# Counting edges on TensorE with the source number split by two bits instead of one

## The reference

```
e = einsum('ehd,ehd->eh', k[src], q[dst]) / sqrt(DK)
m = segment_max(e, dst);  ex = exp(e - m[dst])
z = segment_sum(ex, dst);  attn = ex / z[dst]
a = segment_sum(attn[:, :, None] * v[src], dst)
```

## Time and profile before

| | us |
|---|---|
| median of three runs | 1808.47 |
| lowest and highest run | 1805.55, 1809.08 |
| the profiled execution's own time | 1806.97 |
| its span, first to last instruction | 1805.3 |
| around the span in that execution | 1.67 |
| the stage of the change within the span | 236.4 to 315.9 |
| DVE's first and last one-hot table | 241.67 to 312.50 |
| last product to the end of its logarithm | 314.00 to 315.63 |

### The profile page before, as it was taken

How to read it: one execution, slowest core, us unless ns; L and a number is a source line. 1 busy time by engine, 2 the same in 40 slices (tenths; PEclk the granted TensorE clock), 3 DMA queues, 4 the chain that set the end, 5 groups by cost and what they waited for, 6 DMA issues and landing times. The chain is left out here.

```text
span 1805.3 us, 31339 instructions
## 1 busy us (share of the span) xinstructions
PE 1603.1 (89%) x9860; PEld 1171.5 (65%) x9860; DVE 998.6 (55%) x1981; ACT 732.4 (41%) x1641; POOL 559.7 (31%) x638
## 2 busy tenths in 40 slices
PE   2997857899999887999999999479999999898994
PEld 2555535788888555569999999455555555745662
DVE  7533379788885784610000000469999999441233
ACT  2233346666665234442222211355555555422331
POOL 6777710111100221520000000435555553233133
PEclk7999979899999996999999999679999999998997
DMA  8538810688663304567555550565555554639985
GB/s 208 117 83 267 271 45 1 184 247 234 159 163 85 82 1 175 148 218 290 208 207 205 214 193 9 145 178 163 156 154 155 156 156 112 222 80 279 358 267 185
DMA packets 146055, 305.94 MB, mean 169 GB/s; under 512 B 42493, under 2 KB 59745, under 8 KB 141221
## 3 DMA queue, kind: packets, MB, share of 16 engines
q1 hardware_dynamic: 106590, 224.70, 39.6%
q0 software_dynamic: 39360, 79.86, 16.1%
HBM read 226.47 MB, written 77.96 MB: 169 GB/s over the span
## 5 line engine op out<-in xcount | busy, mean ns | idle before, releaser
L2197 PE MATMUL acc<-prod,ohy 128*64 128x256 f32 x1056 | 248.8, 386 | 7.7 <-DVE prod L2315 7.7
L2241 ACT ACTIVATE ohy<-oh,RECS 128x64 f32<-128x64 f32 x704 | 187.1, 336 | 151.6 <-PE acc L2197 151.5
L2197 PEld LDWEIGHTS acc<-prod,ohy 128*64 128x64 f32 x1056 | 138.4, 138 | 132.3 <-issue 70.7
L2174 POOL DMA_INDIRECT rows<-up_dram,idx x176 | 167.0, 949 | 143.8 <-DVE prod L2315 101.9
L1951 DVE TENSOR_SCALAR FT<-y_ps,b2T 128x188 f32<-128x188 f32 x32 | 13.2, 414 | 323.4 <-PE y_ps L1900 323.4
L321 POOL DMA_INDIRECT rec_dram<-recs,pos x157 | 161.9, 1031 | 60.6 <-issue 49.6
L2200 PE MATMUL acc<-prod,ohy 128*64 128x256 f32 x704 | 177.3, 395 | 0.0
L1888 PE MATMUL hid_ps<-FT,W 128*128 128x188 f32 x1024 | 167.7, 325 | 0.7 <-ACT FT L1925 0.7
L2315 DVE TENSOR_TENSOR prod<-w_ps,rows 128x768 f32<-128x768 f32 x176 | 166.3, 945 | 0.0
L1888 PEld LDWEIGHTS hid_ps<-FT,W 128*128 128x128 f32 x1024 | 165.2, 192 | 0.9 <-issue 0.9
L1900 PE MATMUL y_ps<-hid,W 128*128 128x188 f32 x1024 | 164.5, 323 | 0.0
(11 more groups left out here) (401 smaller groups left out, 2907.8 us busy)
## 6 DMA issues: line engine op xcount, KB each, us to landing
W<-in_L_ffn_w SPq DMA_DIRECT2D x16, 4096.0 KB, 16.6
raw_dram<-X SPq DMA_DIRECT2D x40, 585.9 KB
X<-raw_dram SPq DMA_DIRECT2D x40, 585.9 KB
bankW_sp<-in_L_ffn_W_sp SPq DMA_DIRECT2D x2, 4096.0 KB, 23.3
h_dram<-h3e SPq DMA_DIRECT2D x22, 256.0 KB, 4.8
h<-h_dram SPq DMA_DIRECT2D x22, 256.0 KB
QF<-q_dram SPq DMA_DIRECT2D x20, 250.0 KB, 5.8
b2B<-in_L_ffn_b_sp SPq DMA_DIRECT2D x17, 256.0 KB, 7.6
```

The source lines that it names most:

```text
L2174: pool.indirect_dma_start(out=rows[:, t, :], out_offset=None, in_=up_dram, in_offset=bass.IndirectOffsetOnAxis(ap=idx[:, par, t:t + 1], ax ...
L2197: upper = lambda m: nc.tensor.matmul(acc[0:HALFB, bank, :].rearrange("p (b c) -> p b c", c=MUL)[:, m:4:3 - m, :], ohs[:, 1 + m, :], pr[:, ...
L2241: last = nc.scalar.activation(ohy[:, t % OHY, i, :], oh[:, par, t, :], ACT.Copy, scale=RECS[:, bass.ds(BATCH * g + t, 1), 4 + i])
```

## The change

The source number is split by its two lowest bits instead of its lowest one. There are four classes of sources (`CLASSES = 4`), and each has at most 313 (`FOURTH`). The one-hot of a source has 314 columns instead of 626. The key of a receiver is its place in the block plus 64 times the class, so there are 256 keys instead of 128, and `ohD` has 1024 elements for four tiles instead of 512. PE multiplies the lower 128 keys and the upper 128 keys by the same 313 columns, into the first and the second bank of the region. ACT takes the logarithm in four activations of 313 or 312 columns, each of which writes every fourth column of the masks, and clears 313 columns in each of the two banks.

```diff
-            HALFN = NODES // 2
-            WIDEN = 626
-            PARTS = [(0, 512), (512, HALFN - 512)]
+            CLASSES = 4
+            FOURTH = -(-NODES // CLASSES)
+            WIDEN = FOURTH + FOURTH % 2
...
-                ohS, ohD = sb("ohS", [128, CRING, WIDEN], F16), sb("ohD", [128, CRING // SET, 2 * HALFB, SET], F16)
-                keys_by_tile = sb("keys_by_tile", [128, 2 * HALFB, SET], F16)
+                ohS, ohD = sb("ohS", [128, CRING, WIDEN], F16), sb("ohD", [128, CRING // SET, CLASSES * HALFB, SET], F16)
+                keys_by_tile = sb("keys_by_tile", [128, CLASSES * HALFB, SET], F16)
...
-                            nc.vector.tensor_scalar(parityI[:, mine], srcI[:, mine], 1, None, ALU.bitwise_and)
-                            step(nc.vector.tensor_scalar(srcI[:, mine], srcI[:, mine], 1, None, ALU.arith_shift_right))
+                            nc.vector.tensor_scalar(classI[:, mine], srcI[:, mine], CLASSES - 1, None, ALU.bitwise_and)
+                            step(nc.vector.tensor_scalar(srcI[:, mine], srcI[:, mine], int(math.log2(CLASSES)), None, ALU.arith_shift_right))
...
-                                                    .unsqueeze(1).to_broadcast([128, 2 * HALFB, SET]), ALU.is_equal)
+                                                    .unsqueeze(1).to_broadcast([128, CLASSES * HALFB, SET]), ALU.is_equal)
...
-                                for c0, cn in PARTS:
-                                    last = nc.tensor.matmul(ps[:, bass.ds(spots[t] + c0, cn)], ohD[:, g % AHEAD, :, t],
-                                                            ohS[:, slot, c0:c0 + cn], start=False, stop=False, skip_group_check=True)
+                                for two in range(CLASSES // 2):
+                                    last = nc.tensor.matmul(ps[:, bass.ds(spots[t] + 512 * two, FOURTH)],
+                                                            ohD[:, g % AHEAD, 2 * HALFB * two:2 * HALFB * (two + 1), t],
+                                                            ohS[:, slot, 0:FOURTH], start=False, stop=False, skip_group_check=True)
...
-                            for odd in range(2):
-                                nc.scalar.activation(masks(i)[HALFB * half:HALFB * half + rows, odd:NODES:2],
-                                                     ps[HALFB * odd:HALFB * odd + rows, first:first + HALFN], ACT.Ln,
-                                                     bias=least[HALFB * odd:HALFB * odd + rows, :], scale=4.0).then_inc(logged, 1)
+                            for c in range(CLASSES):
+                                at, own = first + 512 * (c // 2), HALFB * (c % 2)
+                                nc.scalar.activation(masks(i)[HALFB * half:HALFB * half + rows, c:NODES:CLASSES],
+                                                     ps[own:own + rows, at:at + len(range(c, NODES, CLASSES))], ACT.Ln,
+                                                     bias=least[own:own + rows, :], scale=4.0).then_inc(logged, 1)
                             if b + REGIONS < BLOCKS:
-                                act.wait_ge(logged, 2 * (b + 1))
-                                nc.scalar.activation(ps[:, first:first + HALFN], zeros[:, 0:1].to_broadcast([128, HALFN]),
+                                act.wait_ge(logged, CLASSES * (b + 1))
+                                nc.scalar.activation(ps[:, first:first + REGION].rearrange("p (a n) -> p a n", n=512)[:, :, 0:FOURTH],
+                                                     zeros[:, 0:1].unsqueeze(2).to_broadcast([128, 2, FOURTH]),
                                                      ACT.Copy).then_inc(evicted, 1)
```

More of the change, by code:

```diff
@@ L729, in count_edges @@
                 nodes16 = sb("nodes16", [128, WIDEN], F16)
-                srcI, parityI = sb("srcI", [128, ETILES], I32), sb("parityI", [128, ETILES], I32)
+                srcI, classI = sb("srcI", [128, ETILES], I32), sb("classI", [128, ETILES], I32)
                 key16 = sb("key16", [128, GROUPS, EPP], F16)
-                ohS, ohD = sb("ohS", [128, CRING, WIDEN], F16), sb("ohD", [128, CRING // SET, 2 * HALFB, SET], F16)
-                keys_by_tile = sb("keys_by_tile", [128, 2 * HALFB, SET], F16)
+                ohS, ohD = sb("ohS", [128, CRING, WIDEN], F16), sb("ohD", [128, CRING // SET, CLASSES * HALFB, SET], F16)
+                keys_by_tile = sb("keys_by_tile", [128, CLASSES * HALFB, SET], F16)
                 least = sb("least", [128, 1])
@@ L755, in _ @@
                         nc.gpsimd.memset(least[:], 2.0 ** -60)
-                        nc.gpsimd.iota(keys_by_tile[:], pattern=[[1, 2 * HALFB], [0, SET]], base=0, channel_multiplier=0,
+                        nc.gpsimd.iota(keys_by_tile[:], pattern=[[1, CLASSES * HALFB], [0, SET]], base=0, channel_multiplier=0,
                                        allow_small_or_imprecise_dtypes=True)
@@ L779, in keys @@
                             step(nc.vector.tensor_copy(srcI[:, mine], RECS[:, mine, 0]))
-                            nc.vector.tensor_scalar(parityI[:, mine], srcI[:, mine], 1, None, ALU.bitwise_and)
-                            step(nc.vector.tensor_scalar(srcI[:, mine], srcI[:, mine], 1, None, ALU.arith_shift_right))
+                            nc.vector.tensor_scalar(classI[:, mine], srcI[:, mine], CLASSES - 1, None, ALU.bitwise_and)
+                            step(nc.vector.tensor_scalar(srcI[:, mine], srcI[:, mine], int(math.log2(CLASSES)), None, ALU.arith_shift_right))
                             nc.vector.tensor_copy(RECS[:, mine, 0], srcI[:, mine])
                             step(nc.vector.scalar_tensor_tensor(out=key16[:, groups_of, :].rearrange("p g t -> p (g t)"),
-                                                                in0=parityI[:, mine], scalar=float(HALFB), in1=RECS[:, mine, 1],
+                                                                in0=classI[:, mine], scalar=float(HALFB), in1=RECS[:, mine, 1],
                                                                 op0=ALU.mult, op1=ALU.add))
```

## The result

| | us |
|---|---|
| before, median of six runs taken with the changed kernel | 1809.20 (1805.55 to 1812.89) |
| after, median of six runs | 1821.95 (1817.48 to 1826.23) |
| ratio after to before | 1.0077, 95% interval 1.0058 to 1.0097 |
| profiled execution after, its span | 1817.48, 1815.9 |
| length of the stage in the profiled executions | before 79.5, after 94.5 |

A forecast was written before the change was run, and what follows sets the result against it. DVE was taken to set the pace of the stage, PE 16% and ACT about 20% behind. DVE -2.3, PE's end +0.5 and ACT's last block +0.6 sum to -1.2 us: 1807.3 us, range 1804.2 to 1813.

The forecast's parts named there:

- no gain on DVE: Rival: at the lower slope DVE's set stays at 1.51 us; +1.1 us at most, 1809.6; chance 0.15.
- the larger gain: Rival: DVE's set takes 1.35 us, whole 1804, or POOL's stall shrinks, whole 1805; chance 0.13.
- The other form of that rival: POOL's split stalls DVE's last tables 1 us in place of 2.7; sum about -3.4 us, 1805; within the 0.13.
- PE and POOL: PE's products hidden behind DVE by 0.18 us a set; POOL's tables hidden with 2.5 us of cover; stall moves later.
- That term: End of PE's work: last one-hot to last product 2.0 us in place of 1.50; +0.5 us (0 to 1.5).
- ACT: the step that failed: Four logarithms of 0.61 us, a block 3.2 us, absorbed by four regions; only the last block counts, +0.6 us.
- The point of decision: ACT delays DVE's fortieth set, which needs the sixteenth region cleared, from 3.27 us a block, 0.62 us a logarithm.
- the rival: ACT becomes the bound: writes 16 bytes apart cost a second cycle, block 4.1 us; about +13 us, 1821; chance 0.17.
- its mild form: ACT's writes cost half a cycle more: 0.70 us a logarithm, 3.6 us a block; about +3 us, 1811.

The follow-up runs named there:

- experiment 2: Changed kernel with each of the four logarithms writing its columns without a gap (masks' columns in another order): 1804.24 us, ratio 0.9986 to before.
- experiment 3: Changed kernel with the four logarithms writing every second column of half the masks (columns in another order): 1805.04 us, ratio 0.9986 to before.
- experiment 6: Changed kernel with the sources split into four ranges, so each logarithm writes adjacent columns in the right order: 1806.87 us, ratio 0.9995 to before.
- experiment 7: Changed kernel with classes 2k and 2k+1 in two banks, two logarithms a block writing adjacent pairs: 1805.97 us, ratio 0.9989 to before.
- experiment 8: Kernel with sources split into four ranges, its four logarithms reordered 0, 2, 1, 3: 1805.38 us, ratio 0.9994 to before, stage 75.8 us.
- experiment 11: Network left out: four logarithms in a row without waits, same 64 partitions or halves in turns: 1.74 against 2.14 us without a gap.
- experiment 1: Network left out: single activations and copies at several write steps; 313-column logarithm 0.532 us at two words, 0.667 at three, 803 ns at four.
- Experiment 4: Kernel before with its two logarithms a block cut into four writing every fourth column, DVE and PE as before: 1821.88 us, ratio 1.0086.
- experiment 5: Changed kernel with three logarithms writing every third column and the fourth adjacent ones (columns in another order): 1806.82 us, ratio 0.9999 to before.
- experiment 9: Kernel with two logarithms a block writing adjacent pairs, plus POOL waiting for DVE's last one-hot before its split: 1803.97 us, ratio 0.9977 to before.
- experiment 10: Kernel before, plus POOL waiting for DVE's last one-hot before its split of the queries: 1805.13 us, ratio 0.9982.

## Why the prediction was wrong

**DVE: right.** 0.60 us and 0.21 us were forecast for the two tables, a set of 1.45 us; all three were measured. The middle slope, taken between two bounds, was the right one. Where ACT is out of the way (experiments 2, 3, 6 and 7) the stage is 1.1 to 1.7 us shorter, against -1.2. So no gain on DVE falls, and so does the larger gain by a set of 1.35 us. The other form of that rival, a smaller stall by POOL, is not what the changed kernel showed (2.65 us of stall), but experiment 8 had no stall, and its stage was 3.7 us shorter than before.

**PE and POOL: right in kind.** PE's products are hidden behind DVE. POOL's table of keys ended at 239.7, three microseconds ahead of its first use. The stall moved to a later set and the 1.2 GHz stretch to the last products. It was the 42nd set, where the prediction said the 41st or so. That term was too small: the products end 3.4 us behind the last one-hot, where 2.0 was taken, and outside its bounds of 1.5 to 3.0. With ACT out of the way it was 1.4 (experiment 6, stall in the 39th set), 1.9 (3, the 40th) and 2.6 us (2, the 43rd), so it grows as the stall moves to a later set, as the prediction argued.

**ACT: the step that failed.** The prediction gave a logarithm of 313 columns 0.61 us by the slope of the earlier trace rows and a block 3.2 us. Measured were 0.85 us from start to start and 4.12 us. The slope itself is right for writes without a gap, 0.84 ns a column in experiment 11: without a gap or with a step of two such a logarithm takes 0.518 or 0.532 us, in the stage 0.54 and 0.57 from start to start, less than forecast. What failed is that a slope from rows that write dense columns was applied to a write with 16 bytes from one value to the next. The reason that 0.61 was preferred was that a step of 8 bytes cost nothing, and that DVE's L782 ran at a plain rate with 64 bytes. Experiment 1 shows that 8 bytes say nothing of 16: three words cost 149 ns and four 285. DVE's L782 was a stand-in from another engine: its one row has both its widths at the same step, and none without a gap to compare with. In experiment 1 a copy from SBUF to SBUF by DVE pays too, 317 ns without a gap and 434 with a step of four.

**From the term to the time: right.** The point of decision (3.27 us a block), the mechanism (four regions, the fortieth set, grants by POOL's loop) and, to about 2 us of the stage, the rival's sum were right. The rival had the sixteenth region cleared at 313.4 and it was 314.8; 1.0 of that is that ACT began later. Experiment 4 puts ACT's cost into the kernel before and gets the whole slowdown; experiments 2 and 3 take it out and lose it all. At 3.01 us a block, experiment 3, DVE waits for no grant, and at 3.42, experiment 5, for 1.5 us; the point of decision lies between them, where 3.27 had it. Two prices of the rival were too low. The products' end is the one above. And its mild form, 3.6 us a block, was put at about +3 us: by the rival's own steps the sixteenth region is then cleared at 305.4 and the stage ends at 305.4 + 7.3 + 2.7 + 2.0 + 2.8 = 320.2 against 315.6, which is +4.6.

**The chances.** The forecast stood 0.01 us a logarithm from its own point of decision, with no row of ACT for the step of the writes, and called the price of one more cycle improbable at 0.17. The bound of 0.44 to 0.88 us held the true value; the place in it was taken from the wrong rows. The page of the Trainium skill that was cited for the rival (SBUF — State Buffer, Door 1: The DMA port swizzle) pointed the right way for ACT's writes: its lines of 16 bytes fit a cost that is full at four words and stops growing there. Its sentence that 4 fp32 can be strided for free does not fit: three words cost ACT 149 ns and four the full 285. What the Trainium skill says of activations in a row (ScalarE: Activation LUTs, What ACT_TABLE_LOAD costs), an overlap of about 93 ns, agrees with experiment 11 only where the next activation reads the same partitions (0.11 us). The kernel's logarithms take the two halves in turns, and there the row of no overlap was the right one to follow.

What stays open: which part of the path makes the cost. A price for each touched piece of 16 bytes fits the 32-bit rows of experiment 1, but not those of 16-bit values in the last section, and no run here separates the mechanisms that would do that.

## What to carry to other kernels

When a table is split further so that one engine works less, look at how the pieces are put together again: the step of the writes goes with the number of pieces, and the engine that was idle pays for it. If the forecast's margin on a price is a few per cent and no row of that engine shows the operation's step, don't call the dearer price improbable; a small kernel like experiment 1 settles it. Choose the split so that the pieces are ranges or adjacent pairs; it costs a few instructions on the keys and keeps the writes cheap. Here neither gave the whole kernel a gain over the one before that could be told from none.

## What the runs showed of the hardware beyond this

- ACT's write step into SBUF for 16-bit values is dearer still, also against the 0.80 us that had been expected at 16 bytes. Here L81 wrote 313 of them 8 bytes apart and L83 16 bytes apart, where 4 bytes apart took 607 ns:

```profile
L83 ACT ACTIVATE half<-ps,least 64x313 f16<-64x313 f32 x6 | 9.8, 1637 | 0.2
L81 ACT ACTIVATE half<-ps,least 64x313 f16<-64x313 f32 x6 | 5.7, 949 | 0.2
```

- DVE copying 313 columns from PSUM took 477 ns at a step of one and of two words, 698 at four and 671 at sixteen.
- POOL's split of 1000 columns beside DVE's comparisons: in the changed kernel DVE's four tables took 3.58 us in place of 0.93 beside a cast of 1.46 and a subtraction of 2.21. In experiment 8 the cast took 9.68 us and DVE lost nothing. In experiment 2 both happened, one after the other: the cast took 5.84 us with DVE at full pace, and then four tables took 3.60. With POOL's part behind DVE's, the cast took 1.03 us (experiments 9 and 10). Which of these it will be can't be told from the code, and no run here shows what decides it.
